# A decoder layer on one core: another order of the attention iteration on all five queues, earlier loads of x and ctx, entry lists fetched before expert weights

## The reference

```python
# 1: causal self-attention of one head, keys are the normed x itself
scores = einsum('bqe,bke->bqk', xn @ W_qk, xn) / 16 + (kpos - qpos) * slope, causal
x = x + softmax(scores) @ (xn @ W_v.T)
# 2: cross-attention, 16 heads of 16, keys and values from ctx, padding mask
q, k, v = xn2 @ wq.T, ctx @ wk.T, ctx @ wv.T
x = x + (softmax(q k^T / 4, masked) @ v) @ wfc.T
# 3: mixture of experts: 8 experts of width 1024, the two best per token
p = softmax(xn3 @ w_gate); keep top 2, divide by their sum
x = x + sum_e p_e * (silu(xn3 @ Wg_e) * (xn3 @ Wu_e)) @ Wd_e
```

## Time and profile before

| | |
|---|---|
| median of 3 runs | 1168.38 us (1166.47 to 1171.04) |
| profiled execution | 1169.32 us |
| its span, first to last instruction | 1167.2 us |
| busy in the span | PE 1071.1 us, DVE 680.3, ACT 664.1, POOL 524.2 |
| mean granted TensorE clock | 0.982 of full speed |
| iteration 1 begins, iteration 14 begins, last attention begins | 100.1, 511.8, 538.5 us |

### The profile page before, as it was taken

The page is one execution under the profiler, slowest core; times in us unless marked ns, Lnnn a source line. Parts: engine busy times, 40 slices in busy tenths (PEclk is TensorE's granted clock), DMA queues, the critical chain, the costliest instruction groups (busy, mean ns, idle before and its releaser), DMA issues.

```text
span 1167.2 us, 37226 instructions
## 1 busy us (share of the span) xinstructions
PE 1071.1 (92%) x12828; PEld 893.6 (77%) x12828; DVE 680.3 (58%) x2156; ACT 664.1 (57%) x1446; POOL 524.2 (45%) x565
## 2 busy tenths in 40 slices
PE   5689998999998889987899999999999999999996
PEld 4456665666666666653799999999999999999996
DVE  5456767878777777785356444444444444444442
ACT  6468878888887788874443444343443444343442
POOL 5545666666666666643224332322423232333322
PEclk9889999999999999998899999999999999999998
DMA  7445555545566655238622254249222121228321
GB/s 232 153 143 164 157 132 159 161 149 146 156 165 161 171 163 172 91 102 257 236 43 35 38 144 135 36 130 356 37 35 32 32 36 27 36 36 302 77 36 19
DMA packets 91663, 142.66 MB, mean 122 GB/s; under 512 B 20960, under 2 KB 69536, under 8 KB 88288
## 3 DMA queue, kind: packets, MB, share of 16 engines
q1 hardware_dynamic: 75790, 122.95, 34.1%
q0 software_dynamic: 15808, 19.09, 10.1%
q10 hardware_dynamic: 18, 0.01, 0.0%
HBM read 268.13 MB, written 43.47 MB: 267 GB/s over the span
## 4 chain that ended last, share of the span: by engine, by line
PE 55%; DVE 17%; DMA 10%; issue 9%; SPq 4%; POOL 3%; ACT 2%; DVEq 0%; POOLq 0%; ACTq 0%
PE t_ring L1834 15%; PE front L1834 15%; PE pv L1852 8%; PE s_ring L1852 8%; DMA x_in<-in_x 6%; DVE nmax L1096 4%; DMA slot_entry<-entries 2%; DVE xn L1041 2%; DVE stats L1027 2%; PE front L1490 2%; SPq L403 2%; PE s_ring L1477 1%; POOL entries L632 1%; PE pv L1650 1%; PE t_ring L1635 1%
## 5 line engine op out<-in xcount | busy, mean ns | idle before, releaser
L703 POOL DMA_INDIRECT out<-y_sb,place_i x71 | 112.1, 1579 | 321.5 <-DVE y_sb L1386 122.5
L1834 PE MATMUL t_ring<-rows_hi,wgu_sb 128*128 128x128 f16 x2272 | 214.4, 220 | 0.0
L1834 PE MATMUL front<-rows_hi,wgu_sb 128*128 128x128 f16 x2272 | 213.5, 219 | 0.0
L1096 DVE TENSOR_REDUCE nmax<-s_ring 128x2 f32<-128x512 f32 x256 | 164.7, 686 | 70.3 <-PE s_ring L1619 70.2
L1834 PE MATMUL t_ring<-rows_lo,wgu_sb 128*128 128x128 f16 x1136 | 198.5, 220 | 0.0
L1834 PE MATMUL front<-rows_lo,wgu_sb 128*128 128x128 f16 x1136 | 197.6, 219 | 0.0
L839 ACT ACTIVATE probs_t<-t_ring,mask_bias 128x512 f32<-128x512 f32 x256 | 168.9, 689 | 25.2 <-PE t_ring L1635 22.3
L1834 PEld LDWEIGHTS t_ring<-rows_hi,wgu_sb 128*128 128x128 f16 x2272 | 181.2, 98 | 1.6
L1834 PEld LDWEIGHTS front<-rows_hi,wgu_sb 128*128 128x128 f16 x2272 | 180.5, 98 | 2.4 <-issue 0.8
L979 ACT ACTIVATE silu_g<-t_ring 128x256 f32<-128x256 f32 x142 | 54.6, 384 | 167.3 <-PE t_ring L1834 167.3
L657 POOL TENSOR_TENSOR w_halves<-w_scaled,w_halves 128x256 f16<-128x256 f32 x192 | 124.6, 679 | 55.1 <-ACT w_scaled L868 55.1
(11 more groups left out here) (225 smaller groups left out, 2133.8 us busy)
## 6 DMA issues: line engine op xcount, KB each, us to landing
wgu_sb<-gu_split SPq DMA_DIRECT2D x71, 2048.0 KB
wd_sb<-down_split SPq DMA_DIRECT2D x71, 1024.0 KB
w_piece<-in_w_gu SPq DMA_DIRECT2D x32, 512.0 KB, 8.5
gu_split<-w_halves SPq DMA_DIRECT2D x32, 512.0 KB
w_piece<-in_w_down SPq DMA_DIRECT2D x16, 512.0 KB, 9.8
down_split<-w_halves SPq DMA_DIRECT2D x16, 512.0 KB
x_in<-in_x SPq DMA_DIRECT2D x16, 256.0 KB, 7.5
ctx_in<-in_ctx SPq DMA_DIRECT2D x16, 256.0 KB, 7.9
```

The costliest lines, as they stand in the source:

```text
L703: nc.gpsimd.indirect_dma_start(out=out, out_offset=bass.IndirectOffsetOnAxis(ap=place_i[:, j:j + 1], axis=0), in_=y_sb[:, j], in_offset=No ...
L1096: nc.vector.tensor_reduce(nmax[:, n // HJ, :, n % HJ], s_ring[n % 2][:].rearrange("p (r k) -> p r k", r=2), AX.X, ALU.max, negate=True).th ...
L1834: o = nc.tensor.matmul(gu_ring[f][:, part * SLOT:(part + 1) * SLOT], wgu_sb[j][:, w, at:at + P], r[:, j % 2, c], start=(i == 0), stop=(i = ...
```

## The change

SyncE: `load_next(b + 4, p)` replaces `load_next(b + 3, 1 - p)`. It waits for x_res and ctx_t of batch b+2, of the same iteration, and stands behind the stores of the tail and ahead of `store_pieces`, which moves from the end of the iteration to ahead of `stack_rows`; `store_stream` moves to the front. Since b+4 must stay under 16, iterations 11 and 12 are written out and the loop runs 5 times, not 6. At the end of attention the four `entries_at` of slots 4 to 7 stand ahead of the first `load_down` and the loads of experts 1 to 3, not behind them.

GpSimd: the power of the first norm (`rsqrt_norm1`) is parted from `f_norm1`; the three `split_lo` and the norms change places; the scatter also waits for `entry_sb`. ScalarE, TensorE and VectorE: parts in another order. VectorE's helpers are cut into single steps (`moments_of` into `stats_of`, `aggregate`, `variance`; `t_choose`, `t_place` into their instructions), which are placed between the maxima; the second norm has its own `stats2`. What each step computes is unchanged.

```diff
-            with eng.Fori(0, 6) as i:
+            with eng.Fori(0, 5) as i:
                 iteration(2 * i + 1, 1, i, True, True, True, True, True)
                 iteration(2 * i + 2, 0, i + 1, True, True, True, True, True)
+            iteration(11, 1, 5, True, True, True, True, True)
+            iteration(12, 0, 6, True, True, True, True, True)
             iteration(13, 1, 6, True, True, True, True, False)
@@ SyncE @@
             def load_next(n, p):
-                if not isinstance(n, int) or n >= 2:
-                    sp.wait_ge(x1_sb, n - 1)
-                    sp.wait_ge(ctxt_sb, n - 1)
-                    load(n, p)
+                sp.wait_ge(x1_sb, n - 1)
+                sp.wait_ge(ctxt_sb, n - 1)
+                load(n, p)
             def iteration(b, p, h, c, t, s, f, n):
+                if c:
+                    store_stream(b - 1)
                 if n:
-                    load_next(b + 3, 1 - p)
                     load_pieces(b + 3, h + 1 + p, 1 - p)
                 if c:
-                    store_stream(b - 1)
                     store_normed(b - 1, 1 - p)
-                if f:
+                if f and (not isinstance(b, int) or b + 4 < B):
+                    load_next(b + 4, p)
+                if f:
+                    store_pieces(b + 2, h + 1, p)
                     stack_rows(b + 2, p)
-                    stack_k(b + 2, p)
+                    stack_k_hi(b + 2, p)
+                    stack_k_lo(b + 2, p)
                 if s and f:
                     stack_max(b + 1, 1 - p)
                 if f:
                     stack_q_hi(b + 2, p)
                     stack_q_lo(b + 2, p)
-                    store_pieces(b + 2, h + 1, p)
...
             iteration(14, 0, 7, True, True, True, False, False)
+            sp.wait_ge(row_sb, STREAMS)
+            for j in range(STREAMS):
+                entries_at(STREAMS + j, j)
             sp.wait_ge(max_stacked[1], 16 * (B // 2))
             load_down(first, 0)
...
-            sp.wait_ge(row_sb, STREAMS)
-            for j in range(STREAMS):
-                entries_at(STREAMS + j, j)
             iteration(15, 1, 7, True, True, False, False, False)
@@ GpSimd @@
                 if f:
                     xn_rest(b + 2)
+                if c:
+                    out_rest(b - 1)
+                if f:
                     ctx_rest(b + 2)
-                if c:
-                    out_rest(b - 1)
-                if f:
                     split_lo(b + 2, 0)
+                if n:
+                    rsqrt_norm1(b + 3)
                 if c:
                     rsqrt_tail(b - 1)
+                if f:
+                    split_lo(b + 2, 1)
                 if n:
                     f_norm1(b + 3, 1 - p)
                 if f:
+                    split_lo(b + 2, 2)
                     rsqrt_norm2(b + 2)
-                    split_lo(b + 2, 1)
                     xn2_rest(b + 2)
-                    split_lo(b + 2, 2)
                 if c:
                     scatter(b - 1, 1 - p, h)
```

VectorE's iteration 14:

```diff
                 t_norm(b - 1, s_ring[1])
+                early_table(0)
+                t_stream(b - 1)
                 h_max(b + 1, 0, 2)
-                early_table(0)
+                early_table(1)
+                t_norm3(b - 1, 1, b // 2 - 1)
                 h_max(b + 1, 2, 4)
-                early_table(1)
+                early_table(2)
                 h_max(b + 1, 4, 6)
-                early_table(2)
-                t_stream(b - 1)
-                h_max(b + 1, 6, 8)
-                t_norm3(b - 1, 1, b // 2 - 1)
-                h_max(b + 1, 8, 13)
                 t_logits(b - 1)
+                h_max(b + 1, 6, 11)
+                t_choose(b - 1, 1)
+                h_max(b + 1, 11, 13)
+                t_place(b - 1, 1)
                 h_max(b + 1, 13, 16)
                 for j in range(STREAMS):
                     slot_rows(j, j, 0)
-                t_choose(b - 1, 1)
-                t_place(b - 1, 1)
```

442 lines of the change are left out of this document (290 added, 152 removed).

## The result

The changed kernel takes 1122.53 us (median of 4 runs, 1121.08 to 1122.65), the kernel before 1169.23 on the same chip (1166.47 to 1171.04): ratio 0.960, interval 0.958 to 0.962. The profiled execution took 1122.46 us, its span 1120.7, granted clock 0.984.

A forecast was written before the change was run, and what follows sets the result against it. TensorE's products were taken to bound the expert slots, with waits to remove in the iterations and seam. Loop 18, start-up 5, iteration 14 -0.5 and entry lists 7 made 29.5 us off, giving 1140 us; range 1128 to 1152, chance 0.62.

The forecast's parts named there:

- Entry lists: Seam before the expert slots: lists of slots 4 to 7 issued before expert weights end a wait; 7 us gained.
- Start-up: Iterations -2 to 0: v1's projection ahead of p's transposes and x's waits gone; 5 us gained, bounds 0 and 8.
- Item 1: Loop: x loaded four batches ahead, so VectorE's idle time for x goes, 1.4 us an iteration.
- Items 2 and 4: Iteration's start: TensorE waits 0.5 us for ScalarE's ctx copies and 0.6 us for GpSimd's low half of xn.
- Items 3, 5, 6 and 7: Loop: TensorE waits for the maxima's copy 0.3, score work behind ScalarE 0.25, xn2 0.4, chosen 0.75 us an iteration.
- item 3: Iteration's start: the maxima's copy to q_stack lands 2.33 us after issue; TensorE waits 0.3 us, bounds 0 and 5.5.
- item 5: Loop: ScalarE's weight splits stand ahead of p's exponentials and exp(3,0); t_ring is refilled late twice, 0.25 us together.
- Items 6 and 7: Iteration's second half: TensorE waits 0.4 us for xn2, then 0.75 us for chosen and the score group ahead.
- items 2 to 4 hide: Rival: those waits at the iteration's start vanish, loop 29.0 us an iteration, 1123 us; under 1128 us had chance 0.09.
- Iteration 14: Last maxima: VectorE idles 2.3 us for fc, TensorE's chosen wait goes; cost 0.5 us, bounds -2 and +2.
- VectorE as bound: Rival: VectorE's queue keeps iterations at 31.7 us, only seam and start-up gain; 1156 us, 1152 to 1162, chance 0.17.
- the late copy: Rival: the maxima's copy lands behind 1.5 MB of split weights, up to 5.5 us late, 1208 us; slower had chance 0.06.

The follow-up runs named there:

- The loads alone: Kernel before, with SyncE loading x and ctx four batches ahead and iterations 11 and 12 unrolled, no engine's order of work changed: 1172.1 us, ratio 1.008.
- late loads and moments in the new order: Changed kernel, x and ctx loaded three batches ahead, VectorE's moments of x behind f_scores: 1159.3 us; with rsqrt_tail also ahead of rsqrt_norm1: 1145.2 us.
- The experiment that fills this gap: Changed kernel, with five unused subtractions of 256 columns on GpSimd between rsqrt_norm2 and xn2_rest: 1143.8 us, ratio 0.983, on a chip without halts.
- iteration 14 reordered: Changed kernel, in iteration 14 alone: TensorE's xn3 and gate moved, VectorE's early table earlier, gate steps between last maxima: 1120.05 us, ratio 0.963.

## Why the prediction was wrong, by its steps

The gain was 46.7 us, not 29.5. The loop made 19 us of the difference and start-up 1.6; iteration 14 and the last attention took 3.4 back.

**Entry lists** (7 forecast): right, mechanism and size; 7.1 alone, 6.8 in the changed kernel, and no stop or low clock in slot 1.

**Start-up** (5): right in size, 6.6. I put 4 of the 5.5 us down to the order of v1's projection. The loads alone moved iteration 1 by 4 to 7 us, and late loads and moments in the new order lose 5.8 us on one chip, 4.8 on another and 2.7 on a third (98.3 against 95.5), so much of it is the loads': the size was luck in part. The projection's place was not tested.

**Item 1, x** (1.4 us an iteration): a wrong reason. I read VectorE's idle time for x as 1.4 us an iteration to be had by itself; the sum of the new iteration doesn't use it. By itself it was worth nothing or less; other waits took its place. Within the new order early loads and moments together are worth 1.4 us with GpSimd's powers swapped, 2.5 (31.3 against 28.8) without. That the first is the 1.4 of the forecast is luck.

**Items 2 and 4, ctx_h and low xn** (0.5 and 0.6): right, 0.47 and 0.50.

**Items 3, 5, 6 and 7** (0.3, 0.25, 0.4, 0.75): this is the step that failed. They came to nearly nothing, 0.2 us where 1.7 was forecast: the sum of waits is 1.2 us an iteration (28.7 - 27.5), not 2.8. Over thirteen iterations that is 21 us of the gain. The maxima's copy (item 3) lands in 2.0 us where I took 2.33, and held TensorE for 1.0 us in thirteen iterations. For item 5 TensorE waited 0.2 us, once; why was not tested. Items 6 and 7 rested on "VectorE is without a pause" and "their slow forms", that is on its 24.2 us an iteration; it was busy 22.0, and the three slow forms took 0.5 us together, not 1.5. I had read in the earlier trace rows that the one-hot takes 0.55 or 0.19 by what GpSimd does, and said that the chain would be 0.8 us shorter if GpSimd were then elsewhere, but I didn't follow my own walk of GpSimd far enough to see that it stands idle from rsqrt_norm2 at about 20.5 us to xn2_rest at 24.8. The experiment that fills this gap brings back two of the slow forms, VectorE's 23.8 us an iteration and a stop of 1.19 us, and costs 1.7 us an iteration; the one that takes the steps in a block brings back 2.0 us of stop. The rival "items 2 to 4 hide" had the right time (1123) for another reason: 2 and 4 did not hide, 3, 5, 6 and 7 did.

**Iteration 14** (0.5 slower): 3.0 slower. TensorE's busy time there is 2.4 us above that of before at the lower clock (21.30 against 18.87), a term that the forecast doesn't have; the waits in sum account for about 0.6. That this is near my 0.5 is luck, for they are other waits. The stop of 2.16 us for `chosen` went as forecast, but VectorE idled 5.70 us for fc where I had 2.3, and two stops of TensorE came that I had at nothing: 1.85 us for the copy of the maxima and 0.58 for o_nh, with the fall of the clock right behind them. Why the clock fell here stays open: before the change it stayed at 1.00 behind a stop of 2.84 us, and with iteration 14 reordered behind 1.56 and 0.58. Last attention, 0.9 slower, has 1.0 us more busy time of TensorE (24.39 against 23.40) at clock 0.83 against 0.87; it wasn't tested.

**VectorE as bound, and the late copy** as rivals: the first was wrong as a forecast, but 0.2 us of spare at `chosen` (291.98 against 292.17) is all there is. The experiment that makes `chosen` 1.19 us late pays 1.7 us an iteration, the one that makes it 2.0 late at least 1.3. The second did not occur in the loop; the landing that it assumed was about right. Its sum has a slip: the 29 us are lost with 2.3 us more of landing, not 2.8. The chances for faster add up to 0.88, not 0.87.

## What to carry to other kernels

Idle time that one operand causes is no price for removing it: do the removal alone, and see which wait moves up. When an order is walked, walk the engine that shares a resource too, for it decides which of two measured durations an operation will have. And a stage that kept the full clock behind a stop of 2.84 us in one profile may pay for the same stop in the next, up to 3.9 us here.

## What the runs showed of the hardware

Chips differed nearly as much as the change: without halts the kernel before took 1162 to 1169 us, in the three groups with them 1199 to 1205. In the traces of those groups, ScalarE and VectorE stood still for 1 to 4 us near the starts of iterations with their operands ready, and TensorE with them, in part for want of ScalarE's ctx_h; slots were 1% longer too (in the changed kernel TensorE was busy 494.75 of 500 us from 600 us on, against 500.00). The changed kernel's trace there shows the same small instruction loads (31 and 24 packets) as on the first chip. What causes the halts stays open. They hide costs of a microsecond an iteration, so that two costs of 1.4 and 1.7 us an iteration on a chip without them measured as 1 us in the whole kernel.

VectorE's small operations take longer beside GpSimd's: the one-hot 0.19 us with GpSimd idle, 0.54 us in the mean beside its subtractions in the kernel before, and 1.19 us where it began 0.01 us behind one.
